# Sorting the first table of sampled edges earlier, with fewer expert pairs ahead of the edge loop

## The reference, cut to what matters

```
x: 8192 tokens of 256 (LayerNorm in front)
h = x @ W_gat                          # 16 values per token: 4 heads x 4 experts
e = leaky_relu(a_src[src] + a_dst[dst])   # 1048576 edges and one loop per token
alpha = softmax of e over the edges that end in one token
agg = segment_sum(h[src] * alpha, dst) + b_gat
scores = layernorm(agg) averaged over heads; top 2 of 4 experts; softmax -> w
out = sum over the 4 experts of g_e * (gelu(x @ W1[e] + b1[e]) @ W2[e] + b2[e])
```

## Time and profile before

| | |
|---|---|
| median of 3 runs | 4274.07 us (4269.31 to 4278.59) |
| the profiled execution | 4267.88 us, span 4266.1 us |
| PE, DVE, ACT, POOL busy | 83%, 71%, 35%, 32% of the span |
| experts of layer 0, layer 1 | to 2637 us, and from 2884 us to the end |

### The profile page before, as it was taken

One profiled execution on the slowest core, in us unless ns is written; L12 is line 12 of the kernel. 1 busy time (PEld: TensorE's weight loads), 2 busy tenths in 40 slices (PEclk: granted clock), 3 DMA queues, 4 the chain that ended last, 5 costly groups with the idle time before them and its releaser, 6 DMA issues. The chain is left out here.

```text
span 4266.1 us, 51323 instructions
## 1 busy us (share of the span) xinstructions
PE 3538.0 (83%) x17914; PEld 2017.7 (47%) x17914; DVE 3012.3 (71%) x6268; ACT 1493.1 (35%) x2075; POOL 1365.0 (32%) x1016
## 2 busy tenths in 40 slices
PE   5999999999958977888798963786987888799866
PEld 2333333333316643556565642565653555565544
DVE  2676677667748887869993267858887778993357
ACT  2565556556534420222333310313520122233321
POOL 2776676667740000000274521000000000076520
PEclk9999999999978999888899987786999888899988
DMA  3000000000025200000124356126300000024247
GB/s 139 11 30 19 12 30 21 11 31 30 21 83 195 87 27 15 30 30 26 43 58 51 109 203 255 60 67 212 127 37 15 25 25 31 31 58 52 62 173 286
DMA packets 144854, 301.56 MB, mean 71 GB/s; under 512 B 20580, under 2 KB 103140, under 8 KB 139492
## 3 DMA queue, kind: packets, MB, share of 16 engines
q1 hardware_dynamic: 98212, 180.78, 11.8%
q10 hardware_dynamic: 25920, 94.38, 5.8%
q0 software_dynamic: 20480, 23.14, 4.0%
HBM read 183.42 MB, written 114.81 MB: 70 GB/s over the span
## 5 line engine op out<-in xcount | busy, mean ns | idle before, releaser
L1095 PE MATMUL l_pu<-l_tt,l_w 128*128 128x512 f32 x2048 | 1008.3, 617 | 116.4 <-ACT l_hid L1285 103.4
L1106 PE MATMUL l_pd<-l_w,l_hid 128*128 128x256 f32 x4096 | 971.7, 381 | 9.6 <-ACT l_hid L1285 9.6
L1106 PEld LDWEIGHTS l_pd<-l_w,l_hid 128*128 128x128 f32 x4096 | 784.6, 192 | 330.6 <-issue 247.5
L1285 ACT ACTIVATE l_hid<-l_pu,l_b 128x512 f32<-128x512 f32 x512 | 350.1, 687 | 1237.9 <-PE l_pu L1095 1227.8
L1040 POOL DMA_INDIRECT l_g<-hs_rows,l_i_src x336 | 321.6, 957 | 1304.8 <-DVE l_i_src L1655 1203.0
L389 DVE TENSOR_TENSOR at_pr<-at_ps,at_decay 128x1024 f32<-128x1024 f32 x512 | 601.0, 1216 | 177.8 <-PE at_ps L503 176.7
L307 ACT ACTIVATE at_ab<-at_pr 128x1024 f32<-128x1024 f32 x512 | 537.1, 1055 | 436.0 <-DVE at_pr L389 384.7
L258 POOL TENSOR_TENSOR at_ab<-at_ab 128x1024 f32<-128x1024 f32 x256 | 600.8, 2371 | 175.3 <-ACT at_ab L307 175.3
L1095 PEld LDWEIGHTS l_pu<-l_tt,l_w 128*128 128x128 f32 x2048 | 400.3, 200 | 418.3 <-issue 396.6
L503 PE MATMUL at_ps<-at_qr,at_kr 32*128 32x512 f32 x2048 | 348.1, 642 | 13.9 <-issue 9.0
L522 PE MATMUL at_ps_av<-at_pr,at_v 128*32 128x512 f32 x2048 | 272.9, 604 | 6.9 <-ACT at_o L315 5.1
(11 more groups left out here) (341 smaller groups left out, 4216.7 us busy)
## 6 DMA issues: line engine op xcount, KB each, us to landing
ys<-l_yst ACTq DMA_DIRECT2D x112, 512.0 KB, 2.6
l_yb<-ys SPq DMA_DIRECT2D x28, 2048.0 KB, 10.1
l_tt<-tT ACTq DMA_DIRECT2D x36, 512.0 KB, 3.4
at_xt<-in_x SPq DMA_DIRECT2D x16, 1024.0 KB, 5.1
l_xt<-x SPq DMA_DIRECT2D x32, 512.0 KB, 4.1
tT<-l_xnT ACTq DMA_DIRECT2D x32, 512.0 KB, 4.5
l_xo<-x SPq DMA_DIRECT2D x28, 512.0 KB, 4.5
x<-at_xt SPq DMA_DIRECT2D x8, 1024.0 KB, 4.3
```

Of the source, the lines that this page charges most:

```text
L1095: ins = pe.matmul(ps_u[q % 2][:, :], w1[:, e, c, P * q:P * q + P], tt[:, s, c, :], start=(c == 0), stop=(c == KK - 1))
L1106: ins = pe.matmul(out, hid[:, k % 2, c, P * r:P * r + P], w2[:, k % GE, c, :], start=False, stop=(c == MB - 1), skip_group_check=True)
L1285: act.activation(hid[:, k % 2, q, :], ps_u[q % 2][:, :], ACT.Gelu, bias=b1[:, k % GE, q:q + 1]).then_inc(s_act, 1)
```

## The change

- `sort()` for the first table moves from behind the histogram to right behind the number of windows, ahead of rounds three and four.
- `PRE_PAIRS` falls from 48 to 40, so `LOOPED` goes from 8 to 16. The 8 direct pairs stay.
- In the loop PE does 18 quarters ahead of the exchange (`IN_FRONT`), and the rest after it. ACT's two waits come after 20 and 52 quarters instead of 2 and 32.
- `g`, `raw`, `order`, `i_src` and `cf` move in SBUF to where nothing of rounds three and four lies. `code` moves behind the buffers of the node part for that.

```diff
-PRE_PAIRS = PAIRS - 16
+PRE_PAIRS = PAIRS - 24
...
-IN_SCAN = 2
-IN_MERGE = 32
+IN_FRONT = 18
+IN_SCAN = 20
+IN_MERGE = 52
...
             with pe.Fori(0, n) as m:
                 at[0] = 0
+                experts(IN_FRONT, PRE_PAIRS, PRE_PAIRS + LOOPED, m)
                 pe.wait_ge(s_next, m + 1)
...
-                experts(4 * LOOPED + 4, PRE_PAIRS, PRE_PAIRS + LOOPED, m)
+                experts(4 * LOOPED + 4 - IN_FRONT, PRE_PAIRS, PRE_PAIRS + LOOPED, m)
...
             dve.nop().then_inc(s_nwin, 1)
+            sort()
             rounds(ROUNDS1, ROUNDS0)
...
             then(dve.tensor_copy(count[:, :], hist))
-            sort()
```

More of the change, by code:

```diff
@@ L782, in ffn_layer @@
             ic = sb("ic", [P, ECH], I32)
-            code = sb("code", [P, EC], I32)
             picked = sb("picked", [P, LROUNDS * LC])
@@ L792, in ffn_layer @@
             zero = sb("zero", [P, P], BF16)
[L793 to L803, removed]
+            nodes = ExitStack()
+            sb = tensors(nodes)
+            xt = sb("xt", [P, 2, MTT, C])
+            xn = sb("xn", [P, 2, MTT, C])
+            xnT = sb("xnT", [P, 2, KK, MT])
+            stats = sb("stats", [P, MTT, 6])
+            mv = sb("mv", [P, MTT, 2])
+            ve = sb("ve", [P, MTT])
+            sd = sb("sd", [P, MTT])
+            rstd = sb("rstd", [P, MTT])
+            tmp = sb("tmp", [P, MTT, GF])
+            code = sb("code", [P, EC], I32)
+            nodes.close()
             with ExitStack() as hots:
@@ L824, in ffn_layer @@
             res = sb("res", [P, NT, ROWW])
[L825 to L829, removed]
             cb = sb("cb", [P, JT], BF16)
@@ L843, in ffn_layer @@
             fac = sb("fac", [P, GH, JT])
+            g = sb("g", [P, JT, HSW])
+            raw = sb("raw", [P, JT], I32)
+            order = sb("order", [P, JT], I32)
+            i_src = sb("i_src", [P, JT], I32)
+            cf = sb("cf", [P, JT])
         is_col = work[:, :, :].rearrange("p c j -> p (c j)").rearrange("p (j c) -> p j c", c=NT)
```

## The result

The changed kernel takes **4213.49 us** (median of 4 runs, 4212.08 to 4216.11). The kernel before takes 4271.69 us (median of 4 runs, 4267.49 to 4278.59). The ratio is 0.9863, 95% interval 0.9846 to 0.988. The forecast was 4215 us. The profiled execution has a span of 4210.3 us, 55.8 less than before's.

A forecast was written before the change was run, and what follows sets the result against it. No single bound: gathers and PE's front pairs hold the exchange, merge and gates hold PE later. Gains of 31 us (layer 1) and 28 us (layer 0) sum to 59 us, giving a 4215 us median, range 4190 to 4243.

The forecast's parts named there:

- Round three: Sort now before round three: DVE's 6.92 us wait covers part of 17.7 us; the histogram ends 10.8 us later, PE idles.
- Gathers: 168 gathers issued behind the early sort, beside one-hots: end near 3733 to 3846 us, before the exchange's end, cost nothing.
- DVE beside gathers: 40 one-hot instructions beside gathers might cost DVE 0 to 6 us a layer; 0 taken.
- the rival of half the gain eaten: One-hots wait for the port that gathers use: 14 us a layer lost on DVE, 4243 us, chance 0.09.
- The exchange: PE comes at 3876.8 us, waits 5.4 us for DVE's mark; exchange takes 10.4 us, `l_e` starts at 3893 us.
- After the exchange: PE waits 1 us at `l_xm`, 6.43 us for tokens; second direct pair added by 4107 us, 31 us gained.
- ACT's two waits: ACT's second wait, behind 52 quarters, costs DVE about 5 us; gates still ready near 4073 us, no limit.
- Layers: Gain of 31 us in layer 1 and 28 us in layer 0, 59 us in sum.
- The ledger: PE's work unchanged in layer 1: 14.45 + 28.14 us and about 4 us go, 10.8 + 5.4 come, giving 30 us.
- The rival that nothing is gained: PE's idle time only moves, since ACT's three waits stop PE as long as before: 4274 us, chance 0.04.
- the rival of the gates: Direct pairs come early enough, so the gates set the tail: 45.6 us in layer 1, 4186 us, chance 0.10.
- The slower rival: Gathers hold up DVE in the rounds, its work growing by half: 105 us later a layer, 4425 us, chance 0.05.

The follow-up runs named there:

- the run with 10 quarters: The changed kernel with 10 PE quarters ahead of the exchange instead of 18, ACT's waits behind 12 and 44: 4268.52 us, ratio 0.9988 to the kernel before.

## Why the prediction was right

**Round three** (10.8 us to come, DVE's 6.92 us wait to go): the wait is gone. From the unit to the counts are 3690.5 - 3478.7 = 211.9 us now, and 3703.2 - 3501.7 = 201.4 before: 10.4 came. The windows of that stretch, before and after, show that PE has the same number of records in it and 8.8 us more of idle time; the rest is 2.2 us more of work, at a granted clock of 0.82 instead of 0.84:

```profile
3502.00:3703.00 201.00, 155.40 (x1026) 109.85 (x1024) 180.98 (x391) 46.31 (x72) 0.00 (x0) 0.84 0.09 32
```

```profile
3479.00:3691.00 212.00, 157.64 (x1026) 111.66 (x1025) 197.16 (x456) 46.33 (x72) 154.35 (x126) 0.82 0.16 37
```

**Gathers** (end 210 to 280 us behind the sort, cover 47 us or more, cost 0): they take 245.8 us and end 125.0 us before `l_e`, and half as many again cost nothing. The bound by POOL standing still for 65.4 us of one-hots was nearly twice too high: 245.8 - 210.7 = 35.1 us are lost to them.

**DVE beside gathers** (0 taken, of 0 to 6): 0. The one-hots' means agree within 2 ns, the 64 MAX8 of the two rounds take 415 ns instead of 409, 0.4 us in all, and the rival of half the gain eaten (14 us a layer) is out on this chip. The row with two SBUF inputs was the right neighbour, and the one of 0.44 us wasn't.

**ACT's exponential** (DVE waits some 15 us): 15.31.

**The exchange** (PE waits 5.4 us; 10.4 us long; `l_e` at 3893 us): PE comes at 3853.73 + 23.07 = 3876.8 us, as forecast, the wait is 3.28 us, and `l_e` comes at 3869.13 + 23.07 = 3892.2 us by before's clock.

**After the exchange** (1 us at `l_xm`, 6.43 for tokens, the second direct pair added 31 us earlier): 1.55 us, 6.39 us, and 31.2 us. The gates come at 4050.9 + 23.1 = 4074 us, forecast 4073, and DVE waits 11.20 us for the first direct pair, forecast 12.

**ACT's two waits** were undersized in one place: DVE stands 6.98 us for the scan's exponential instead of before's 2.75. It cost nothing, as the gates had 11 us of room.

**Layers** (31 and 28 us): 32.7 and 27.5. The 31 us are reached at the second direct pair, and the tail behind it, taken as unchanged, adds 1.5.

**The ledger** (30 us in layer 1: 42.6 of waits and 4 of slow restarts go, 16.2 come). The windows from the unit to the second direct pair, before and after:

```profile
3502.00:4138.00 636.00, 536.04 (x2328) 356.72 (x2327) 433.48 (x769) 190.79 (x289) 243.30 (x235) 0.90 0.25 63
```

```profile
3479.00:4084.00 605.00, 536.06 (x2329) 357.36 (x2328) 433.28 (x769) 189.69 (x289) 278.31 (x235) 0.92 0.23 64
```

PE's work is the same to 0.02 us, and its idle time falls from 100.0 to 68.9 us, which is the whole gain of 31 us. So the mechanism is as forecast, and the run with 10 quarters confirms it. But two of its sizes were off against each other: less idle time came than the 16.2 us (8.8 up to the counts and 1.7 from there to the exchange's end), and the 4 us of slow restarts didn't show in PE's work as a whole. That the sum is right within 1 us is luck in this.

The rival that nothing is gained and the rival of the gates are out on this chip: the gates had room until nine more of PE's quarters were moved into its idle time. The slower rival was given 0.05 and dismissed by two rows of one trace. Two chips show its kind of effect, which no row of before, taken on a chip without it, could.

## What to carry to other kernels

Price a move by the idle time of the engine whose work bounds the stretch, and add what the same move brings: here two halves that are worth 0 and -28 us alone gave 58 together. Then look down that engine's timeline for idle time that no change has touched; the quarters moved into round three and the leftover loop, with ACT's exponential two quarters behind the histogram, gave about 50 us, nearly as much as the change itself. A time on one chip isn't the time on all: measure a kernel with many indirect gathers on more than one before trusting a gain of one per cent.

## What was not expected of the hardware

Beside DVE's one-hot instructions a gather takes 3.03 us instead of 0.94, one for each chunk of 3.34 us (15 of the 20 chunks have one of 2.8 us or more), and DVE isn't slowed (2129 ns against 2128). So only one side pays here. By the Trainium skill, SBUF — State Buffer, section "SBUF: two separate sides", whichever of a GpSimd operation and a DVE instruction of certain kinds (in a 2-port mode or, against a GpSimd operation that reads SBUF, with two SBUF inputs) starts first gets the shared port pair for the whole instruction, and the other fully blocks. The trace agrees for gathers behind DVE. For the other order it has these two rows, and there DVE doesn't wait:

```profile
3522.23 1.09 POOL L1042 DMA_INDIRECT l_g<-hs_rows,l_i_src  x1 [0.30 <-issue]
```

```profile
3522.54 2.29 DVE L1480 TENSOR_TENSOR l_one_lo<-l_iota,l_lo 128x4096 bf16<-128x4096 bf16 x1
```

The gather has run for 0.31 us when the one-hot begins, and the one-hot has its usual length. At which moment of its 1.09 us a gather uses the port isn't shown, nor in which mode the one-hots run.

On two of the chips PE, DVE and ACT start instructions at a fraction of their rate while gathers are issued, 1.1 to 1.2 us lost for each gather, and POOL alone isn't held up. On the others no such thing is seen, with 252 gathers either.
